# An eight-stage transformer megakernel on one core: key turning three steps late, summaries selected instead of multiplied, a projection between scores and transposed heads, and the first feed-forward tile readied early

## The reference, cut to what matters

```python
# x: (8, 100, 512); ctx: (8, 361, 512); 16 heads
x = x + L0_xattn(layernorm(x), ctx); x = x + L0_ffn(layernorm(x))     # grouped heads; 16 experts
x = x + L1_xattn(layernorm(x), ctx); x = x + L1_ffn(layernorm(x))
x = x + L2_xattn(layernorm(x), ctx)      # a scan over ctx; its mean is one summary row for each sequence
x = x + L2_ffn(layernorm(x))
x = x + L3_xattn(layernorm(x), ctx); x = x + L3_ffn(layernorm(x))

def L2_xattn(Z, kv):                     # per sequence
    x = kv @ W_in.T + b_in; states = scan(s = K*s + x)
    summary = mean(states @ W_out.T + b_out, axis=time)       # (1, 512)
    return layernorm(Z + summary) * gamma + beta

def L3_xattn(x, ctx):                    # 257 image keys and 104 text keys, softmax over each apart
    q = rms_norm(x @ q_w.T + q_b); k, v for the image part and the text part, k rms-normed
    out = softmax(q k_txt) v_txt + softmax(q k_img) v_img     # 16 heads of 32
    return out @ o_w.T + o_b

def L3_ffn(x, w1, w2, w3):               # quant: groups of 64 along a row, 8 bits
    w' = sign(w) * mean(|w|)             # one scale for each weight matrix
    h = silu(quant(x) @ w1'.T) * (quant(x) @ w2'.T)
    return quant(h) @ w3'.T
```

## Time and profile before

| | us |
|---|---|
| median of 3 runs | 2762.11 (2761.98 to 2762.43) |
| profiled execution, time | 2760.57 |
| profiled execution, span | 2758.7 |
| PE busy | 2497.6 (91%) |
| DVE, ACT, POOL busy | 1403.2, 817.8, 795.2 |

### The profile page before, as it was taken

One profiled execution on the slowest core, in us unless ns is written; L12 is line 12 of the kernel. 1 busy time (PEld: TensorE's weight loads), 2 busy tenths in 40 slices (PEclk: granted clock), 3 DMA queues, 4 the chain that ended last, 5 costly groups with the idle time before them and its releaser, 6 DMA issues. The chain is left out here.

```text
span 2758.7 us, 31937 instructions
## 1 busy us (share of the span) xinstructions
PE 2497.6 (91%) x10778; PEld 1335.7 (48%) x10798; DVE 1403.2 (51%) x3518; ACT 817.8 (30%) x2121; POOL 795.2 (29%) x776
## 2 busy tenths in 40 slices
PE   7999999979989998999789898799988888886998
PEld 3445555544455655555455555444433444443444
DVE  4543333123211324676567676775743554555786
ACT  1134443212211114555430101311103454453332
POOL 2655444111200004321123233200002454553333
PEclk9999999989989998999769999999998999997999
DMA  6014000021185632110232223600003111110000
GB/s 174 1 72 156 14 19 4 1 76 36 48 299 188 208 144 77 51 37 16 72 131 95 89 91 126 222 2 8 8 8 97 53 49 34 49 27 32 6 8 12
DMA packets 86883, 195.81 MB, mean 71 GB/s; under 512 B 18379, under 2 KB 35179, under 8 KB 84431
## 3 DMA queue, kind: packets, MB, share of 16 engines
q1 hardware_dynamic: 80590, 180.79, 19.6%
q0 software_dynamic: 6144, 13.13, 1.7%
HBM read 150.32 MB, written 38.60 MB: 68 GB/s over the span
## 5 line engine op out<-in xcount | busy, mean ns | idle before, releaser
L3178 POOL TENSOR_SCALAR a_p<-a_p,a_li 100x257 f32<-100x257 f32 (+1 forms) x256 | 186.6, 750 | 181.1 <-DVE a_li L3064 181.1
L2850 PE MATMUL bank<-l_early,a_ctx 128*128 128x512 f32 (+1 forms) x384 | 188.8, 639 | 7.5 <-DVE a_pt L3069 7.4
L632 POOL TENSOR_SCALAR a_shared<-a_shared,a_li 128x361 f32<-128x361 f32 x104 | 131.6, 1265 | 201.8 <-DVE a_li L537 201.8
L2303 PE MATMUL bank<-f_xT,s_w 128*128 128x400 f32 x512 | 181.0, 508 | 1.3 <-ACT f_xT L2327 1.3
L1937 PE MATMUL bank<-s_wgu,f_xT 128*128 128x512 f32 x384 | 168.9, 593 | 0.7 <-ACTq L2113 0.7
L2303 PEld LDWEIGHTS bank<-f_xT,s_w 128*128 128x128 f32 x512 | 99.0, 194 | 78.1 <-issue 5.6
L1937 PE MATMUL bank<-s_w,f_xT 128*128 128x512 bf16 x564 | 129.4, 383 | 5.7 <-POOLq L2080 5.0
L1660 POOL DMA_INDIRECT a_got<-slots_y,slots_of x32 | 33.8, 1056 | 292.7 <-POOLq L998 283.9
L2850 PEld LDWEIGHTS bank<-l_early,a_ctx 128*128 128x128 f32 (+1 forms) x384 | 71.6, 196 | 95.2 <-issue 88.5
L1937 PEld LDWEIGHTS bank<-s_wgu,f_xT 128*128 128x128 f32 x384 | 72.7, 190 | 92.2 <-issue 90.5
L334 PE MATMUL bank<-a_wv,a_ctx 128*128 128x512 f32 (+1 forms) x192 | 93.5, 608 | 9.3 <-DMA a_wv<-in_L_xattn_Wv 9.3
(11 more groups left out here) (417 smaller groups left out, 5151.4 us busy)
## 6 DMA issues: line engine op xcount, KB each, us to landing
f_triple<-in_L_ffn_triples SPq DMA_DIRECT2D x16, 768.0 KB, 4.2
rounded<-f_triple SPq DMA_DIRECT2D x16, 768.0 KB, 3.3
s_whole<-in_L_ffn_w SPq DMA_DIRECT2D x24, 512.0 KB, 3.8
e_wg<-in_L_ffn_w_gate SPq DMA_DIRECT2D x16, 704.0 KB, 4.5
e_wu<-in_L_ffn_w_up SPq DMA_DIRECT2D x16, 704.0 KB, 6.1
slots_x<-zero SPq DMA_DIRECT2D x4, 2304.0 KB, 16.4
e_xg<-slots_x SPq DMA_DIRECT2D x16, 512.0 KB, 5.4
e_wd<-in_L_ffn_w_down SPq DMA_DIRECT2D x16, 512.0 KB, 4.2
```

Source lines behind the costliest of these rows:

```text
L632: pool.tensor_scalar(p[s % NP], p[s % NP], li[:, b % 2, h:h + 1], None, ALU.mult).then_inc(normed, 1)
L2303: mm = nc.tensor.matmul(banks[f % 2][:, 0:GT], w[:, kc, f * P:(f + 1) * P], xT[:, kc, :], start=(kc == 0), stop=(kc == KC - 1))
L2850: mm = nc.tensor.matmul(bank[0:m, :], columns[:, kc], w[:, kc, :], start=(kc == 0), stop=(kc == KC - 1))
L3178: pool.tensor_scalar(p[g % 2][j][:, lo:hi], p[g % 2][j][:, lo:hi], li[:, h, i:i + 1], None, ALU.mult) \
```

## The change

Five parts. (1) In stage L0 the turning of a key unit moves one step later (`LAG` 3 in place of 2) on PE and ACT; DVE's scaling stays. (2) In the L2 recurrence the product of `u` and `wout` is made once for all eight sequences (4 matmuls, 8 rows, copied out by ACT), and one matmul with a one-hot matrix `each` spreads the row of one sequence over 100 rows; `broadcast` goes. (3) In L3 attention PE gets a projection between `scores` and `turn_heads` in three of four groups, `values(n, 2)` moves ahead of `scores(n, 0)`, `project_out(b-1)` moves to the fourth group, DVE does all maxima, then the inverses, then the copies of a group, and the bias of the output goes to POOL. (4) In the last sequence DVE sums the magnitudes of the last eight pieces, and measures, normalizes and quantizes the feed-forward's first tile, which PE turns and ACT and POOL split; `project_out(7)` comes after the product that totals the sums. (5) `stage_ffn` takes that tile as `lead`, starts with its `gate_up`, and takes the tiles in order, tile 6 last.

```diff
+    LAG = 3
-            if b + 1 < B and h >= 2:
-                turns += [("k", b + 1, UNITS[u][1]) for u in DONE[h - 2] if UNITS[u][0] == "k"]
+            if b + 1 < B and h >= LAG:
+                turns += [("k", b + 1, UNITS[u][1]) for u in DONE[h - LAG] if UNITS[u][0] == "k"]
...
@@ stage_ffn
-                turn_x(0)
+                if not lead_by:
+                    turn_x(0)
                 gate_up(0)
                 turn_x(1)
...
-              quantize_group, GROUP, [...], out, last_rows, (0, 6, 1, 2, 3, 4, 5))
+              quantize_group, GROUP, [...], out, last_rows, range(len(TILES)), third.x0)
...
@@ stage_L2_recurrence
-                def broadcast(i):
-                    if i >= 2:
-                        dve.wait_ge(got, i - 1)
-                    dve.tensor_copy(ub[i % 2][:], u[:, :, ORDER[i]:ORDER[i] + 1].to_broadcast([P, KC, S])).then_inc(ub_made, 1)
+                def summaries():
+                    pe.wait_ge(u_made, KC)
+                    for kc in range(KC):
+                        mm = nc.tensor.matmul(k.bank[1][0:B, :], u[:, kc, :], wout[:, kc, :], start=(kc == 0), stop=(kc == KC - 1))
+                    mm.then_inc(all_made, 1)
+                def summary(i):
+                    if i == 0:
+                        pe.wait_ge(each_made, 1)
+                        pe.wait_ge(all_copied, 1)
+                    if i >= 2:
+                        pe.wait_ge(got_read, i - 1)
+                    nc.tensor.matmul(g_bank[i % 2][0:S, :], each[:, ORDER[i], :], all8[:], start=True, stop=True).then_inc(got, 1)
+                summaries()
...
@@ stage_L3_attention, SP
+                    if i >= BOTH + 4:
+                        sp.wait_ge(signed, i - 3)
+                        sp.wait_ge(last_pieced, i - 3 - BOTH)
...
@@ stage_L3_attention, PE
                     scores(b, 1)
+                    if more:
+                        keys(n, 0)
                     turn_heads(b, 0)
                     if more:
-                        keys(n, 0)
+                        keys(n, 1)
                         turn_x(n)
-                    if b > 0:
+                    else:
                         project_out(b - 1)
                     outputs(b, 0)
-                    if more:
-                        keys(n, 1)
                     scores(b, 2)
+                    if more:
+                        keys(n, 2)
                     turn_heads(b, 1)
                     if more:
-                        keys(n, 2)
                         queries(n)
                     outputs(b, 1)
+                    scores(b, 3)
                     if more:
                         values(n, 0)
-                    scores(b, 3)
+                    else:
+                        turn_first_tile()
                     turn_heads(b, 2)
...
                         turn_keys(n)
                         turn_queries(n)
+                        values(n, 2)
                         scores(n, 0)
                     turn_heads(b, 3)
-                    if more:
-                        values(n, 2)
+                    if more and b > 0:
+                        project_out(b - 1)
                     outputs(b, 3)
-                project_out(B - 1)
-                pe.wait_ge(pieced, 3 * PIECES)
+                pe.wait_ge(pieced, BOTH)
+                pe.wait_ge(last_pieced, PIECES)
                 pe.wait_ge(exped, B * NH)
                 nc.tensor.matmul(s_bank[0][:, 0:3 * PIECES], k.ones[:], third.sums[:], ...)
+                project_out(B - 1)
...
@@ stage_L3_attention, DVE (the loop as it is after the change)
+                    all_maxima(b, 1)
+                    inverses(b, 1)
                     if more:
                         add_bias(n, 0)
+                    copy_heads(b, 0)
                     if more:
                         add_bias(n, 1)
+                    else:
+                        add_output(b - 1)
+                        measure_first_tile()
+                        sum_pieces(BOTH, 2)
+                    all_maxima(b, 2)
+                    inverses(b, 2)
                     if more:
                         add_bias(n, 2)
+                    copy_heads(b, 1)
                     if more:
                         add_query_bias(n)
+                    else:
+                        round_first_tile()
+                        sum_pieces(BOTH + 2, 1)
+                    if b + 2 < B:
+                        measure(b + 2)
+                    all_maxima(b, 3)
                     if more:
                         mean_squares(n)
+                    inverses(b, 3)
+                    copy_heads(b, 2)
                     if more:
                         scale_keys(n)
+                        copy_keys(n)
+                    else:
+                        sum_pieces(BOTH + 3, 5)
+                    copy_heads(b, 3)
                     if more:
+                        all_maxima(n, 0)
+                        if b > 0:
+                            add_output(b - 1)
                         inverses(n, 0)
...
@@ stage_L3_attention, ACT (in the groups)
                     exponentials(b, 1)
                     if more:
-                        copy_x(n)
                         squares(n, 0)
                         squares(n, 1)
+                        copy_x(n)
                     signs(b, 0)
                     exponentials(b, 2)
                     if more:
                         squares(n, 2)
-                        copy_values(n, 0)
                         query_squares(n)
                     signs(b, 1)
                     exponentials(b, 3)
                     if more:
+                        copy_values(n, 0)
                         copy_values(n, 1)
                         copy_keys(n)
+                        copy_values(n, 2)
                         exponentials(n, 0)
-                        copy_values(n, 2)
+                    else:
+                        take_first_tile()
                     signs(b, 2)
+                round_rest()
```

More of the change, by code:

```diff
@@ L1854, in stage_ffn @@
         LT = BF16 if scales else F32
+        lead_by = 1 if lead is not None else 0
+        nth = lambda i: i + 1 - lead_by
         NT = len(turns)
@@ L1863, in stage_ffn @@
         var, rstd = sb("var", [P, NT]), sb("rstd", [P, NT])
-        xn, xT = sb("xn", [P, D]), [sb(f"xT{i}", [P, N, KC, P], LT) for i in range(2)]
+        xn, xT = sb("xn", [P, D]), [lead if lead_by and i == 0 else sb(f"xT{i}", [P, N, KC, P], LT)[:] for i in range(2)]
         sg, h = [sb(f"sg{i}", [P, D]) for i in range(2)], [sb(f"h{i}", [P, D]) for i in range(2)]
@@ L2061, in _ @@
                             add(n)
-                add(NT - 1)
+                for n in range(NT):
+                    if last[n] + 2 + (n == tail) >= U:
+                        add(n)
             @program.gpsimd
@@ L2529, in stage_L2_recurrence @@
         m, u = k.ctx_sum, sb("u", [P, KC, B])
-        ub = [sb(f"ub{i}", [P, KC, S]) for i in range(2)]
+        each, all8 = sb("each", [B, B, S]), sb("summaries", [B, D])
         added = sb("added", [S, D])
@@ L2818, in _ @@
                 for b in range(B):
+                    for i in sent[b, 0]:
+                        piece(i)
                     if b + 2 < B:
@@ L2841, in _ @@
                                     if seq == n:
[L2842 to L2843 removed]
+                                        sp.dma_start(third.rows[at:at + m, tile, :], k.res[s:s + m, n, :]) \
+                                            .then_inc(moved if tile else first_moved, 16)
+                sp.wait_ge(moved, 16 * sum(seq < B - 1 for tile in range(1, len(TILES)) for seq, *_ in tile_pieces(tile)))
             @block.tensor
@@ L2939, in outputs, with turn_first_tile @@
                         mm.then_inc(summed, 1)
+                def turn_first_tile():
+                    pe.wait_ge(x0_made, 1)
+                    pe.wait_ge(*R.free("x0"))
+                    for kc in range(KC):
+                        mm = nc.tensor.transpose(R.bank("x0")[:, kc * P:(kc + 1) * P], x0[:, kc * P:(kc + 1) * P], k.ident[:])
+                    mm.then_inc(R.fills("x0"), 1)
                 def project_out(b):
@@ L3000, in _, with sum_pieces @@
                 step = Link(dve, stepped)
+                def sum_pieces(first, n):
+                    for i in range(first, first + n):
+                        dve.wait_ge(piece_in[i % 4], (i // 4 + 1) * 16)
+                        dve.tensor_reduce(third.sums[:, i:i + 1], third.whole[i % 4][:], AX.X, ALU.add,
+                                          apply_absolute_value=True).then_inc(last_pieced, 1)
                 def measure(b):
@@ L3123, in _ @@
                 copy_keys(0)
-                for j in range(GH):
-                    maxima(0, 0, j)
+                all_maxima(0, 0)
                 inverses(0, 0)
```

198 lines of the change are left out of this document (113 added, 85 removed).

## The result

The changed kernel takes 2735.7 us (median of four executions, 2733.6 to 2740.1) against 2762.3 before: a ratio of 0.9906, 95% interval 0.9889 to 0.9923, so 26.6 us less (21 to 31). The forecast was 2736. The profiled execution has a span of 2731.8 us, against 2758.7. So totals are compared by medians, and what one stage gains is read from the profiled executions: the moment at which a stage's first product starts, minus that of the stage before.

The account below looks back on a forecast made before the run. PE, busy for 91% of the span, was taken to bound the kernel. The terms -19 - 4.5 + 3 - 1.5 - 4 gave -26 us, span 2758.7 to 2732.7, so a time of 2736 us; range 2714 to 2752.

Parts of the forecast that it names:

- Part 1: L0 attention: 21 waits of PE for scaled key rows go with later turning; -19 us, bounds -19.5 and 0.
- Rival D: L0 attention: scaled rows are late again a step later, so no gain there; total 2755 us, chance 0.06.
- Part 2: L2 recurrence: shorter DVE periods, and PE's turnings resume earlier; -4.5 us, bounds -6.5 and +1.
- the L2 feed-forward keeps its order: 0: L2 feed-forward, behind the recurrence: its order stays, so its time was to change by 0.
- Part 3: L3 attention's steady sequences: new order saves PE's idle time, loses it where ACT has pieces; +3 us, bounds -8, +12.
- The group costs: L3 attention: what each group costs over PE's work, with pieces: 1.85, 3.2, 2.05 and 0.1 us.
- Rival B: L3 attention: the clock falls in two groups of each sequence, +7 us over the forecast there; total 2743, chance 0.20.
- Rival A: L3 attention: copies keep pace with turning, idle time and slow product go; total 2691 us, chance 0.10.
- Rival E: L3 attention: ACT's queue bounds, exponentials wait behind pieces, each wait sets the slow clock; total 2771 us, chance 0.02.
- Part 4: Last L3 attention sequence: readied tile saves 15.8 us, DVE's work pays back 14; -1.5 us, bounds -6 and +4.
- rival C: Last L3 attention sequence: DVE's additions are hidden, which gives -14 us there; total 2723, chance 0.12.
- Part 5: Last feed-forward: first to sixth product 7.5 us shorter, some given back later; -4 us, bounds -7.5 and -1.

Follow-up runs that it names:

- three: Kernel before the change, with only its new L2 recurrence added; 2758.1 us against 2761.5, ratio 0.9986.
- four: Changed kernel with ACT taking the first feed-forward piece ahead of the second key chunk's squares and the second ahead of the query's squares; 2698.7 us, ratio 0.9764.
- eight: Changed kernel with DVE's eight last-sequence sums moved to where DVE waits: four before adding sequence 6's output, four during the last projection; 2723.5 us, ratio 0.9868.
- ten: Changed kernel with the short tile 6 second in the last feed-forward, as before, in place of last; 2738.8 us, ratio 0.9918.
- e4_sums: Changed kernel with DVE's eight sums of the last sequence moved to where DVE waits; 2723.5 us, ratio 0.9868.
- e11_lag2: Changed kernel with the L0 key turning back at two steps, all other parts kept; 2757.7 us against 2762.2, ratio 0.9984.
- e12_first: Changed kernel with only the first feed-forward piece of a sequence moved, ahead of the squares of the second key chunk; 2709.3 us, ratio 0.9811.
- e6_order: Changed kernel with the short tile 6 second in the last feed-forward in place of last; 2738.8 us, ratio 0.9918.
- e3_pieces: Changed kernel with both feed-forward pieces of a sequence moved earlier in ACT's queue, ahead of squares; 2698.7 us, ratio 0.9764.

## Why the prediction came out right

**The sum** was right to 1 us of the span (-26.9 against -26), but that is partly luck, since errors cancel: 3.7 us more in L0 and 1.9 in stages that nothing touched stand against 2.5 lost behind the recurrence, 1.4 at the attention's entry and 0.9 and 1.0 in parts 3 and 5. The entry took either 43.5 or 44.9 us in the runs, with either kernel's order; its first product, 8.38 us before and 9.71 after, is the clock's.

**Part 1** (-19): -22.7. The mechanism holds, the term was mis-sized. I took the idle time in the table of waits for the whole price of a wait; it was 1.13 us per wait, not 0.91, since each one also breaks the overlap of 0.2 us. Rival D is refuted by the single wait of 0.8 us that is left.

**Part 2** (-4.5): -5.2 here, -4.7 alone. The step that failed is "the L2 feed-forward keeps its order: 0". I had named the clock for the turnings only, where it struck in six of the eleven executions with the new recurrence (three); and in six of them the next stage lost 2.0 to 2.7 at its two ends.

**Part 3** (+3): +3.9. The forecast's terms don't give its own sum: 42.8 + 1.85 + 1.3 + 0.75 + 0.1 is 46.8, not 46.5, and with pieces and clock it is 51.7 to 53.4, so the part comes to about +5. The group costs were 1.3, 3.0, 2.0 and 0, where I had 1.85, 3.2, 2.05 and 0.1. Of the sequences with pieces, those from 2 to 4 took 52.0, 51.6 and 53.1 us, inside 51.4 to 53.2; sequence 5 took 49.1 (I had 50.0), sequence 6 45.3 (46.2). The first group was the one over-costed: its maxima start 0.6 us later than the 0.9 of an undelayed chain, and its inverses end at 5.6 us, not 5.9.

I missed that sequence 0 has no out-projection in its fourth group: PE comes 3.65 us earlier to the scores of sequence 1, waits 0.67 us for copies and then, score by score, for the exponentials of the heads before, whose banks they take: 3.1 us of waits in ACT's pace, so that the four scores take 3.88 us in place of 1.07. Behind them the key projection runs at the slow clock (6.08 us, granted clock 0.60), and sequence 1 comes to 56.6 us, 5.5 more than before. Without this the seven sequences would have come to -1.6, so that +3.9 lies close to +3 is luck.

Rival B's condition, two slow products in a sequence, did occur in four of the five, yet the part didn't get its +7, as the waits themselves were shorter than forecast and sequences 5 and 6 gained 5.0 and not 3.2; and its cause could be taken away (four), so it was never a bound of the new order. The loop that pays the slow clock anew in each iteration is what the Trainium skill describes ("TensorE: Matmul & The Clock Gate", section "HAM oscillation — how this bites in real kernels"); the trace agrees, with products of 5.0 to 6.3 us behind the waits of groups 2 and 3 (there PE waits for a DMA, here for other engines to empty its banks).

Rival A (2691) is nearly what the pieces' edit reached (2698.7): the argument against it, in-order queues, was right of this kernel, but the place of a piece in its queue was free to choose. Rival E (0.02) had the wrong size and much of the right mechanism: the exponentials of groups 2 and 3 do stand behind a piece, and the waits that follow do set the slow clock, which the moved pieces took away. It was ACT's order, with ACT busy for 26 us of a sequence in either kernel, not its work.

**Part 4** (-1.5): -1.9. First product 52.4 us after the first scores (I had 53), maxima of group 2 at 17.0 (16.8), of group 3 at 28.4 (28.6), sums at 1.15 to 1.22 us, far from the bound of 1.9, and done at 41.7 (42.4), the projection from 45.5 (46.3) at 5.47 us. Four of the eight sums cost nothing when they stand in a wait of 5.24 us that the same trace shows (eight), so rival C was false of this kernel; with a few lines moved, 7 to 9 of its 12.5 us came true.

**Part 5** (-4): -3.0. First to sixth product 39.4 us, not 37.8 (45.35 before): the steps were 6.8, 6.9, 9.2, 8.2 and 8.2 us where I had 6.9, 5.9, 8.6, 8.2 and 8.2, the second and third mis-sized, the second because PE also waits 1.10 us there for DVE's hidden rows. Of this 3.0 came back later (I had 3.6). The reason I gave for the order was incomplete: its worth is 8 us with the readied tile, most of it the transfer of the last rows that it hides (ten).

## What to carry to other kernels

A queue's position matters where its engine is idle half the time: look for the engine's own waits (ACT's of 4.6 and 7.2 us here) and put optional work into those, not behind the last thing done; two places moved gave more than the whole change. Count a removed wait of a pipelined engine with the overlap that it breaks, 0.2 us on top of each idle figure here. And try a new order together with what stands in its way, since neither of the two may show anything alone.

## What the runs showed that I had not expected

- The slow clock came behind waits that differ little: behind 1.28 us (and behind 0.69 + 0.49) the next product always took 3.65 to 3.70 us; behind 2.03 us it took 5.2 to 5.3 in sequences 0, 1, 2 and 4, and not in sequence 3, in the changed kernel, in e4_sums, e11_lag2 and e12_first alike; in e6_order, with the same attention, sequence 4 was spared too (3.62 us behind 2.02). Behind 2.34 and another 0.4 to 0.7 us it always took 4.9 to 6.4. So the length of the wait doesn't settle it. What PE did in between decides too, which these runs don't resolve: behind the scores of sequence 1, made in 3.88 us with 3.1 of waits in five pieces, the product took 6.08.
- The releaser that the profile names can be the wrong one where an instruction waits for two: 17.6 us stand under POOL's normalized heads in the table of waits; 14.0 of them (six of 2.34 us, in group 2) went with two entries moved in ACT's queue, and in e3_pieces 3.6 are left there, those of the last sequence.
- The clock moves microseconds between stages from one execution to the next: recurrence and feed-forward took 69.2 + 287.7, 73.3 + 284.9 and 73.3 + 288.2 us, with the same code for both. A gain of 5 us read from one stage of one execution can be 2 in the next.
